# Copying the rows of x to the output in 64 small transfers instead of eight large ones

## What is computed

```python
xn = layernorm(x)
phi_q, phi_k = elu(xn @ Wq.T + bq) + 1, elu(xn @ Wk.T + bk) + 1
v = xn @ Wv.T + bv
s = (phi_q * cumsum(phi_k * v, axis=1)) * SCALE @ Wo.T + bo
# top 2 of 8 experts per token, at most 256 tokens an expert;
# all experts share w1, w2
g = silu(sum over kept choices of prob * (gelu(xn @ w1.T + b1) @ w2.T + b2))
out = x + s * g
```

## Time and profile before

| | |
|---|---|
| median of 3 runs | 2103.1 us (2100.84 to 2108.29) |
| the profiled execution | 2110.36 us, span 2108.6 us |
| PE busy | 1992.3 us, 94% of the span |
| DVE, ACT, POOL busy | 66%, 33%, 23% |
| HBM read and written | 206 GB/s over the span |

### The profile page before, as it was taken

How to read it: one execution, slowest core, us unless ns; L and a number is a source line. 1 busy time by engine, 2 the same in 40 slices (tenths; PEclk the granted TensorE clock), 3 DMA queues, 4 the chain that set the end, 5 groups by cost and what they waited for, 6 DMA issues and landing times.

```text
span 2108.6 us, 27175 instructions
## 1 busy us (share of the span) xinstructions
PE 1992.3 (94%) x9380; PEld 906.9 (43%) x9380; DVE 1391.7 (66%) x2092; ACT 692.0 (33%) x1098; POOL 477.5 (23%) x576
## 2 busy tenths in 40 slices
PE   8779999999989889999999999979999999999996
PEld 2234444445434334444444444434444444444442
DVE  3688888888878667567667767576544554545455
ACT  1322222322464433433443443342222122212222
POOL 0188888888700010000000010020000000000002
PEclk9899999999999999999999999999999999999998
DMA  8676666667997876766776675984433333333326
GB/s 300 238 229 210 218 212 225 232 208 219 297 374 251 244 255 217 246 191 223 241 235 215 230 254 177 336 236 128 161 121 101 104 96 106 104 101 99 101 90 140
DMA packets 179223, 419.88 MB, mean 199 GB/s; under 512 B 17776, under 2 KB 72624, under 8 KB 177328
## 3 DMA queue, kind: packets, MB, share of 16 engines
q1 hardware_dynamic: 141488, 291.60, 42.3%
q0 software_dynamic: 29024, 117.51, 17.6%
q10 hardware_dynamic: 8608, 9.44, 1.4%
HBM read 268.51 MB, written 166.77 MB: 206 GB/s over the span
## 4 chain that ended last, share of the span: by engine, by line
PE 72%; DVE 9%; DMA 8%; issue 5%; ACT 3%; SPq 1%; DVEq 1%; ACTq 0%; POOL 0%; POOLq 0%
PE pair L1830 34%; PE pair L1800 23%; PE pair L1722 12%; DMA arena<-up_sums 4%; PE pair L1654 2%; DMA arena<-x_t 2%; PE pair L1695 1%; DMA xraw_dram<-xnT 1%; DVE arena L1156 1%; PE pair L1731 1%; ACT arena L893 1%; DVE xnT L440 1%; DVE arena L1162 1%; DMA arena<-up_dram 1%; ACT arena L969 1%
## 5 line engine op out<-in xcount | busy, mean ns | idle before, releaser
L1830 PE MATMUL pair<-arena 128*128 128x512 f16 x3360 | 729.5, 379 | 4.8 <-DVE arena L1495 1.5
L1800 PE MATMUL pair<-xnT,arena 128*128 128x512 f16 x2400 | 537.7, 384 | 46.8 <-ACT arena L956 12.8
L1830 PEld LDWEIGHTS pair<-arena 128*128 128x128 f16 x3360 | 328.1, 98 | 403.2 <-issue 9.1
L1500 DVE SCALAR_TENSOR_TENSOR arena<-pair,arena 128x1024 f32<-128x1024 f32 x234 | 286.2, 1223 | 166.8 <-PE pair L1830 166.3
L1722 PE MATMUL pair<-arena 128*128 128x512 f16 x1728 | 385.2, 380 | 10.8 <-DVE xnT L440 10.8
L1800 PEld LDWEIGHTS pair<-xnT,arena 128*128 128x128 f16 x2400 | 235.3, 99 | 342.9 <-issue 24.4
L969 ACT ACTIVATE arena<-arena 128x512 f16<-128x512 f32 x280 | 170.1, 626 | 580.6 <-PE pair L1830 516.6
L1722 PEld LDWEIGHTS pair<-arena 128*128 128x128 f16 x1728 | 168.8, 98 | 207.0 <-issue 17.8
L1800 PE MATMUL pair<-xnT 128*128 128x512 f16 x960 | 213.7, 379 | 0.0
L1476 DVE SCALAR_TENSOR_TENSOR arena<-arena 128x512 f16<-128x512 f32 x280 | 189.2, 684 | 16.3 <-ACT arena L969 15.0
L755 POOL DMA_INDIRECT meta_dram<-meta,slot_i x32 | 34.4, 1074 | 524.3 <-PE pair L1830 516.7
(11 more groups left out here) (197 smaller groups left out, 1760.9 us busy)
## 6 DMA issues: line engine op xcount, KB each, us to landing
down_dram<-arena SPq DMA_DIRECT2D x70, 512.0 KB, 4.1
arena<-down_dram SPq DMA_DIRECT2D x70, 512.0 KB, 3.2
up_dram<-arena SPq DMA_DIRECT2D x100, 256.0 KB, 4.7
arena<-up_dram SPq DMA_DIRECT2D x100, 256.0 KB, 2.6
arena<-w_up POOLq DMA_DIRECT2D x40, 512.0 KB, 5.4
up_sums<-arena POOLq DMA_DIRECT2D x40, 512.0 KB, 3.6
arena<-w_down POOLq DMA_DIRECT2D x40, 512.0 KB, 5.1
down_sums<-arena POOLq DMA_DIRECT2D x40, 512.0 KB, 4.6
```

Source lines behind the costliest of these rows:

```text
L1500: ins = nc.vector.scalar_tensor_tensor(to, src, scale, to, ALU.mult, ALU.add)
L1800: ins = mm(out_to, w[:, a, c * P:(c + 1) * P], x_in_op[:, b, c, :], start=(first and i == 0), stop=(i == 11), skip_group_check=True)
L1830: ins = mm(bank[2 + t // 2][:, (t % 2) * BLOCK:(t % 2 + 1) * BLOCK], g_ops[:, A_NAMES.index(DOWN_A[j]), c, a, t * P:(t + 1) * P], down_rin ...
```

## The change

The eight copies of 2 MB, each described as 32 rows of 64 KB spread over 16 parts, become 64 copies of 256 KB. Copy p of group n takes 64 rows that lie eight rows apart, each row a piece of 4 KB. It is issued when product min(p, 6) of down n is done, and not when the whole down is. The four scatters of a group are spread in the same way over its first four products. The waits for `meta_ready` and `meta_filled` are moved ahead of the loop. In group 1 the four pieces of `save_s` now come after the group's copies and scatters, all four behind the end of the down; in the second half they are where they were. The final wait for the copies counts 64 in place of 8.

```diff
-            def save_s(n):
+            def save_s(n, sums):
                 half = n // GROUPS
-                for c, added in ((C11, 4), (C12, 10), (C22, 12), (C21, 14)):
+                for c, added in sums:
                     pool.wait_ge(down_added, 14 * n + added)
...
+            out_rows = out.rearrange("(n r p) d -> n p r d", n=8, p=8)
+            x_rows = x.rearrange("(n r p) d -> n p r d", n=8, p=8)
+            pool.wait_ge(meta_ready, 1)
+            pool.wait_ge(meta_filled, 16)
             for n in range(8):
+                for p in range(8):
+                    pool.wait_ge(down_done, 28 * n + 4 * min(p, 6) + 4)
+                    if p < 4:
+
+                        t = 4 * n + p
+                        pool.indirect_dma_start(
+                            meta_dram, bass.IndirectOffsetOnAxis(ap=slot_i[:, t:t + 1].bitcast(U32), axis=0),
+                            meta[:, t, :], None, bounds_check=SLOTS - 1, oob_is_err=False).then_inc(meta_stored, 16)
+                    pool.dma_start(out_rows[n, p], x_rows[n, p]).then_inc(copied, 16)
                 if n == ATT_GROUPS - 1:
-                    save_s(n)
-
-                if n == 0:
-                    pool.wait_ge(meta_ready, 1)
-                    pool.wait_ge(meta_filled, 16)
-                pool.wait_ge(down_done, 28 * (n + 1))
-                for t in range(4 * n, 4 * n + 4):
-                    pool.indirect_dma_start(
-                        meta_dram, bass.IndirectOffsetOnAxis(ap=slot_i[:, t:t + 1].bitcast(U32), axis=0), meta[:, t, :],
-                        None, bounds_check=SLOTS - 1, oob_is_err=False).then_inc(meta_stored, 16)
-                pool.dma_start(out.rearrange("(n a r) d -> n a (r d)", n=8, a=16)[n],
-                               x.rearrange("(n a r) d -> n a (r d)", n=8, a=16)[n]).then_inc(copied, 16)
+                    save_s(n, FIRST_SUMS + LAST_SUMS)
...
-            pool.wait_ge(copied, 16 * 8)
+            pool.wait_ge(copied, 16 * 64)
```

More of the change, by code:

```diff
@@ L743, in save_s @@
                       .then_inc(s_stored, 16)
-            for n in range(8):
-                if n == ATT_GROUPS - 1:
-                    save_s(n)
-                if n == 0:
-                    pool.wait_ge(meta_ready, 1)
-                    pool.wait_ge(meta_filled, 16)
-                pool.wait_ge(down_done, 28 * (n + 1))
-                for t in range(4 * n, 4 * n + 4):
-                    pool.indirect_dma_start(
-                        meta_dram, bass.IndirectOffsetOnAxis(ap=slot_i[:, t:t + 1].bitcast(U32), axis=0), meta[:, t, :],
-                        None, bounds_check=SLOTS - 1, oob_is_err=False).then_inc(meta_stored, 16)
-                pool.dma_start(out.rearrange("(n a r) d -> n a (r d)", n=8, a=16)[n],
-                               x.rearrange("(n a r) d -> n a (r d)", n=8, a=16)[n]).then_inc(copied, 16)
+            FIRST_SUMS, LAST_SUMS = ((C11, 4), (C12, 10)), ((C22, 12), (C21, 14))
+            out_rows = out.rearrange("(n r p) d -> n p r d", n=8, p=8)
+            x_rows = x.rearrange("(n r p) d -> n p r d", n=8, p=8)
+            pool.wait_ge(meta_ready, 1)
+            pool.wait_ge(meta_filled, 16)
+            for n in range(8):
+                for p in range(8):
[6 more added lines that the diff above has]
+                    pool.dma_start(out_rows[n, p], x_rows[n, p]).then_inc(copied, 16)
+                if n == ATT_GROUPS - 1:
+                    save_s(n, FIRST_SUMS + LAST_SUMS)
             pool.wait_ge(meta_stored, 16 * TILES)
@@ L771, in _ @@
             pool.wait_ge(meta_loaded, 16)
-            pool.wait_ge(copied, 16 * 8)
+            pool.wait_ge(copied, 16 * 64)
             for half in range(HALVES):
                 if half:
-                    save_s(GROUPS + ATT_GROUPS - 1)
+                    save_s(GROUPS + ATT_GROUPS - 1, FIRST_SUMS + LAST_SUMS)
                 for i in LAST_TILES if half else range(HALF_TILES):
```

## The result

The changed kernel takes 2081.2 us (median of 4 runs, 2077.0 to 2084.7) against 2104.4 us before (4 runs). The quotient of the two medians is 0.9890; the ratio on record is 0.9869, with a 95% interval of 0.9847 to 0.9891, so the kernel is faster by 1.1 to 1.5%. 2079.2 us were forecast. The profiled execution took 2079.2 us, its span 2077.5 us; 2086.5 us were forecast against the profile before.

The account below looks back on a forecast made before the run. PE bounds the kernel; in eight groups it loses 31.9 us waiting behind late loads held up by 2 MB copies. With 8.0 us left, the gain is 23.9 us: 2103.1 - 23.9 = 2079.2 us median, range 2070 to 2094 us.

Parts of the forecast that it names:

- 31.9 us in eight groups: First half, groups 0 to 7: 612.1 us against 580.2 us for clean groups, the most a cure there can return.
- The copies' price: 64 small copies, mostly within the downs: 0.8 us of all engines each, 6.3 us a group, nothing charged to PE.
- the bounds of 0.6 and 4.7: Per small copy: 0.6 us at the best rate of 442 GB/s, 4.7 us if engines are held until a 256 KB landing.
- a sign that it is wrong altogether: Any of: PE idle within a down, small copies above 1 us of all engines, same ACT waits with no copy near.
- small transfers fill the engines: Slower rival: above 3.7 us a small copy the weight stream falls behind in every group; at 4.7 us, 2142 us; chance 0.04.
- 5.6 us a group: Spill from downs into quads if the eight small copies' estimated 20.8 us held the engines; the forecast did not charge it.
- 3.0 + 2.0 + 6 x 0.5 = 8.0 us: Losses left: 3.0 us in group 0, 2.0 in group 1, 0.5 in each of groups 2 to 7.
- the 0.81 us: PE's wait mid-group from group 4 on; in group 4 the chain leads back to a 7.79 us load; most should go.
- Group 1's stores: Four attention-result stores moved to about 765 us, behind group 1's last copies; group 1 was taken to keep 2.0 us.
- the prediction's own sign for that: Stores priced too cheap if group 1 is above 75 us with ACT waiting for a load between 765 and 785 us.
- the attention quad: Quad ahead of group 0; such quads make PE wait with no copy near, 3.06 us; group 0 keeps 3.0 of 10.2 us.
- The innocent-copy rival: Loads of sums are late by themselves, so PE's waits stay or return elsewhere: 2097 to 2109 us, chance 0.07.

Follow-up runs that it names:

- The pieces alone: Kernel before, each 2 MB copy still one transfer at the down's end but in 4 KB pieces: ratio 0.9951 to before, eight groups 602.7 us.
- The place alone: Kernel before, 2 MB copy in 64 KB pieces issued behind each down's first product, not its last: ratio 0.9871 to before, eight groups 584.4 us.
- the addresses: Kernel before, group n copying rows of group (n + 4) mod 8: groups 82.6, 81.6, 77.6, 77.3, 73.9, 73.4, 73.8, 73.8 us (one execution).
- a carried backlog: Kernel before, copies of groups 0 and 1 issued behind their downs' first product: groups 75.2, 73.2, 78.3, 76.4, 74.1, 73.7, 73.5, 73.9 us (one execution).

## Why the prediction was right, point by point

- **What the losses were.** 31.9 us in eight groups, from waits for ACT and a lower clock behind three of them, was read rightly: all but 5.3 us went, and the clock is 1.00 in every group. That the copies made them is shown by the kernels that only move them: 612.1 us become 584.4.
- **The copies' price.** Nothing for PE was right: without copies the groups take no less, and with twice as many 2.7 us more. The share in the down was forecast as 0.75 and is 0.72. The engine time was sized too low: 0.8 us a copy was taken, between the bounds of 0.6 and 4.7, and the rows give 0.9 to 1.7 us, 7.4 to 13.9 us a group in place of 6.3. The prediction named more than 1 us a copy as a sign that it is wrong altogether. In group 2 it is 1.7 us, and PE is busy there in all of 72.5 us; so the sign was badly chosen, since the time that engines spend on a copy is not the time that PE waits. The rival "small transfers fill the engines" falls; its bound of 3.7 us a copy is not reached. The Trainium skill's rule of at least 1 MiB per DMA ("DMA: Bandwidth & Descriptors", "Rules for kernel authors") came, by the prediction's estimate, to 5.6 us a group. Measured is nothing (585.5 us with the copies, 586.0 without). Nor does the rule stand against the large copies issued early, which do as well (584.4 us).
- **The sum.** Left in the groups were 3.0 + 2.0 + 6 x 0.5 = 8.0 us by forecast, and 2.7 + 2.7 + 0 by measurement. Groups 2 to 7 were oversized by 3 us: I left 0.5 us each although the chain already led the 0.81 us back to the copy. Group 1's stores were undersized by 0.7 us, and the prediction's own sign for that came up: group 1 is above 75 us, and ACT waits for loads behind the burst.

```profile
767.17 0.63 ACT L887 ACTIVATE arena<-arena 128x512 f16<-128x512 f32 x1 [2.95 <-DMA arena<-up_sums]
...
771.22 0.63 ACT L887 ACTIVATE arena<-arena 128x512 f16<-128x512 f32 x1 [1.28 <-DMA arena<-up_sums]
```

  That the stores and not the attention work make group 1's loss is now shown. Group 0's rest is there with no copy at all; that the attention quad makes it, as the prediction says, fits and was not tested.
- **The number and luck.** 2079.2 us were forecast and 2081.2 measured, closer than such medians can tell: the four runs span 7.7 us. The groups gained 26.6 us where 23.9 were forecast, the medians 23.2, the two profiled executions 31.1. That the errors in the sum (3 us too much left, 0.7 too little) hardly show in the median is luck.
- **The mechanism was right in its core and too simple in two places.** The prediction named the size of the piece, beside which SP's packets pass, and the place, in the quads. The pieces alone bring 9.4 us of 26.6. The place alone brings all of it, and so does spreading small copies over the very quads in which the large one did harm. What hurts is 2 MB queued at one moment ahead of the quads' loads. Either cure is enough, and the change applied both. Spread copies that keep pieces of 64 KB were not run, so how much of the second cure is the spreading and how much the small pieces stays open.
- **The innocent-copy rival** had for it that groups 4 to 7 hardly lost. That remains unexplained, though two readings of it, the addresses and a carried backlog, were tested and fell. The rival itself falls: the same copies, moved, leave groups 2 to 7 without a wait.

## What to carry to other kernels

When a background copy costs time, look at which loads are issued in the few microseconds around it and who waits for them, not at the average DMA share. Here engines at a share of 0.87 cost PE nothing, and one lump of 6 us of engine time at a share of 0.79 cost up to 7.5 us (10.2 in group 0, less the 2.7 that are there without it). First try issuing the lump at a moment whose loads have slack (one moved wait did it here); cut it into small transfers where there is no such moment. And count every other bulk transfer near it: in group 1 the stores, not the copies, set what was left. Lastly, the time that engines spend on a transfer is no price by itself: in group 2 the copy's rose from 7.8 us (10.0% of 78.2 us) to 13.9 while the group got 5.7 us shorter.

## What the runs showed of the hardware

A copy within DRAM in 64 KB pieces keeps the other queues' packets from starting for some microseconds at a time: in the earlier trace rows and in the early copy's slices nothing starts in gaps of 1.25 to 2.5 us, two in each. I had expected pieces of 4 KB to end that harm by themselves, but with 2 MB of them queued a load of 256 KB still took 12.9 us. A small copy's engine time is not fixed: 0.9 us in group 6 and 1.7 us in group 2, its scatter included. And twice the copies, 16 of 256 KB in a group at 265 GB/s in all, left PE without one idle microsecond in six of eight groups.
